# Attention's value product: values stationary in column groups, float32 probabilities moving

## The reference

```
def xattn(q, k, v, ...):            # q = layernorm(x), k = v = ctx; B=4, T=512
    q, k = rms_norm(q), rms_norm(k)
    # 16 query heads, 4 key/value heads (groups of 4 heads), head width 32; rotary embedding
    scores = einsum('bgnqd,bgkd->bgnqk', qg, k) / sqrt(32)
    scores = where(causal, scores, -1e30)
    attn = softmax(scores, axis=-1)
    out = einsum('bgnqk,bgkd->bgnqd', attn, v)
    return out @ w_out.T
x = x + xattn(layernorm(x), ctx)
x = x + ffn(layernorm(x))           # router, top 4 of 128 experts mixed from 8 bases, shared part
```

## Time and profile before

| | us |
|---|---|
| median of 3 runs (lowest, highest) | 987.56 (986.49, 988.49) |
| the profiled execution | 985.09 |
| its span in the trace | 983.3 |
| busy: PE, PEld | 863.3, 695.6 |
| busy: DVE, ACT, POOL | 566.4, 373.6, 355.8 |

### The profile page before, as it was taken

How to read it: one execution, slowest core, us unless ns; L and a number is a source line. 1 busy time by engine, 2 the same in 40 slices (tenths; PEclk the granted TensorE clock), 3 DMA queues, 4 the chain that set the end, 5 groups by cost and what they waited for, 6 DMA issues and landing times.

```text
span 983.3 us, 15430 instructions
## 1 busy us (share of the span) xinstructions
PE 863.3 (88%) x5008; PEld 695.6 (71%) x5008; DVE 566.4 (58%) x1406; ACT 373.6 (38%) x700; POOL 355.8 (36%) x384
## 2 busy tenths in 40 slices
PE   0488868986989986479999999999999999999998
PEld 0256656775777765368888888888888887888886
DVE  4487999899898876457644434343343434333332
ACT  1046867685687784155322212122121212111111
POOL 5746988778887334000012222222222220000000
PEclk9998988998997996879999999999999999999999
DMA  6311231231231200101011101010110100000000
GB/s 176 78 45 42 71 106 42 59 91 32 55 73 39 77 2 0 54 1 44 1 42 66 43 1 43 1 43 1 44 43 1 43 1 11 22 25 30 22 33 33
DMA packets 32814, 40.28 MB, mean 41 GB/s; under 512 B 6496, under 2 KB 19424, under 8 KB 32736
## 3 DMA queue, kind: packets, MB, share of 16 engines
q1 hardware_dynamic: 32736, 39.29, 13.9%
HBM read 19.08 MB, written 4.19 MB: 24 GB/s over the span
## 4 chain that ended last, share of the span: by engine, by line
PE 70%; DVE 14%; issue 7%; SPq 3%; ACT 2%; DMA 2%; POOL 1%; DVEq 0%; ACTq 0%; POOLq 0%
PE pair L1366 22%; PE bank L1366 22%; PE bank L1430 7%; PE bank L1308 5%; PE bank L1240 3%; DVE bank L940 3%; DVE p_l L959 3%; PE bank L1287 3%; SPq L378 2%; PE bank L1389 1%; SPq L365 1%; DVE mx L940 1%; PE pair L1255 1%; PE bank L1377 1%; PE bank L1444 1%
## 5 line engine op out<-in xcount | busy, mean ns | idle before, releaser
L645 POOL TENSOR_TENSOR macc<-macc,gb 128x256 f32<-128x256 f32 x112 | 85.8, 766 | 317.9 <-DVE gb L1160 317.9
L1240 PE MATMUL bank<-k_st,q_st 96*128 96x256 f32 (+2 forms) x256 | 98.2, 438 | 48.4 <-DVE mx L940 42.7
L940 DVE CUSTOM_DVE_ANT_0 bank<-bank,mask_qk 128x128 f32<-128x128 f32 (+3 forms) x256 | 121.1, 507 | 21.2 <-PE bank L1240 19.8
L1366 PE MATMUL pair<-w_h,t_h 128*128 128x512 f32 x320 | 126.7, 396 | 0.0
L1366 PE MATMUL bank<-w_h,t_h 128*128 128x512 f32 x320 | 126.6, 396 | 0.0
L1366 PE MATMUL pair<-w_l,t_h 128*128 128x512 f32 x320 | 125.7, 393 | 0.0
L1366 PE MATMUL bank<-w_l,t_h 128*128 128x512 f32 x320 | 125.6, 393 | 0.0
L1366 PE MATMUL pair<-w_h,t_l 128*128 128x512 f32 x320 | 125.6, 393 | 0.0
L1366 PE MATMUL bank<-w_h,t_l 128*128 128x512 f32 x320 | 125.6, 393 | 0.0
L959 DVE TENSOR_TENSOR p_l<-p,p_h 128x896 f16<-128x896 f32 x96 | 109.2, 1143 | 0.0
L1147 DVE SCALAR_TENSOR_TENSOR ga<-th,pair 128x256 f32<-128x256 f32 x80 | 33.6, 420 | 126.5 <-ACT th L800 126.5
(11 more groups left out here) (178 smaller groups left out, 1858.2 us busy)
## 6 DMA issues: line engine op xcount, KB each, us to landing
q_st<-turned_h SPq DMA_DIRECT2D x128, 64.0 KB, 2.0
q_st<-turned_l SPq DMA_DIRECT2D x64, 64.0 KB, 2.0
raw<-in_L_ffn_w_gate SPq DMA_DIRECT2D x16, 256.0 KB, 2.8
raw<-in_L_ffn_w_up SPq DMA_DIRECT2D x16, 256.0 KB, 3.6
out<-x SPq DMA_DIRECT2D x16, 256.0 KB, 2.0
x<-in_x SPq DMA_DIRECT2D x3, 1024.0 KB, 5.8
k_st<-turned_h SPq DMA_DIRECT2D x32, 64.0 KB, 2.0
ct<-in_ctx SPq DMA_DIRECT2D x4, 256.0 KB, 2.9
```

Of the source, the lines that this page charges most:

```text
L645: e.tensor_tensor(macc[:, g, :], macc[:, g, :], gb[:, i % 2, :], ALU.add).then_inc(s_acc, 1)
L940: e.tensor_tensor_reduce(s[:, 0:width], s[:, 0:width], mask_qk[:, T - width:T], 1.0, -3e38, ALU.add, ALU.max, mx[:, c % 2, t, j:j + 1]).th ...
L1240: e.matmul(a_bank[i % 2][:, 0:w], q_st[0:MAXROW, c % QR, j, t * P:(t + 1) * P], k_st[0:MAXROW, c % KR, 0:w], start=True, stop=True).then_i ...
L1366: last = e.matmul(g_bank[n % 4][:, 0:2 * I], t[:, k, cols], ww[:, k, :], start=(k == 0 and m == 0), stop=(k == KC - 1 and m == 2))
```

## The change

The probabilities are kept in float32 and not split. V, also float32 and straight from the loaded context, is the stationary operand, 128 keys x 32 columns, and the probabilities move, up to 512 columns at a time. The four heads of a group write four different quarters of the partitions of one bank, so the result comes out already turned; `combine` and `turn_out` are gone. The product is made once for a group of four heads, in one piece of 16 matmuls, at tick (c + 1) * G + 1. The row sums come from pass A: after the row minimum (scores now carry the sign and the scale, so minima stand for maxima) ScalarE takes the exponential of the score tile in its bank with an accumulator. The bank is free only then; there are three instead of two. The reciprocals are spread over 32 columns each by GpSimd, turned by TensorE, copied out by ScalarE, and multiplied on VectorE. Projections alternate between two banks and stand two to a tick. The context of all batches is loaded once, at the start, with x.

```diff
-LOW_BEHIND = 1
-PV_BEHIND = 2
+PV_TICK = 1
+    AR = 3
+    PW = G * (XW + YW + P)
+    def prob_at(k, j):
+        return (j * XW, j * XW + T, G * XW + j * YW, G * (XW + YW) + j * P)[k]
-        a_bank = bank[0:2]
-        b_bank = bank[2]
-        v_bank = bank[3]
+        a_bank = bank[0:3]
+        b_bank = bank[3]
+        o_bank = bank[5]
+            for b in range(2, B):
+                load_ctx(b)
+                load_x(b)
...
+            def out_low(c):       # GpSimd
+                e.tensor_tensor(o_l[:, kv, :], att[:], f32(o_h[:, kv, :]), ALU.subtract).then_inc(s_ol, 1)
+            def spread_inverse(c):
+                e.tensor_copy(heads(rrep[:]), rinv[:, c % 2].unsqueeze(3).broadcast_to([P, TT, G, D])
+                              ).then_inc(s_rrep, 1)
...
-            def exps(n, name):
+            def row_sum(n, t):    # ScalarE
+                s = a_bank[i % AR][:, 0:width]
+                e.wait_ge(s_max, i + 1)
+                e.activation(s, s, ACT.Exp, bias=mx[:, c % 2, t, j:j + 1], scale=-1.0,
+                             accum_out=sums[:, c % 2, t, j:j + 1]).then_inc(s_sum, 1)
+            def inverse_out(c):
+                e.activation(r_t[:, c % 2, :], m_bank[0][:], ACT.Copy).then_inc(s_rout, 1)
+            def exp_x(n):
+                e.activation(pr[:, c % 2, j * XW:(j + 1) * XW], pair[:, 0:XW], ACT.Exp, scale=-1.0
+                             ).then_inc(s_ex, 1)
+            def exp_y(c, y):
+                e.activation(pr[:, c % 2, at:at + T], b_bank[:], ACT.Exp, scale=-1.0).then_inc(s_ey, 1)
-            def value_rows(n):
+                if 0 <= n < NH:
+                    exp_x(n)
+                if 0 <= ahead < NH:
+                    row_sum(ahead, 0)
+                    row_sum(ahead, 1)
...                 # turned_high
+                if 0 <= n < NH and n % G < 3:
+                    exp_y(n // G, n % G)
+                if 0 <= ahead < NH:
+                    row_sum(ahead, 2)
+                    row_sum(ahead, 3)
+                for c in range(NC):
+                    if n == c * G + AT["maxima_turned"] + 1:
+                        inverse_out(c)
+                    if n == (c + 1) * G + PV_TICK:
+                        out_high(c)
...             # VectorE: maxima_split moves to the start of the next tick
+                e.wait_ge(s_sum, (c + 1) * G * TT)
+                e.reciprocal(rinv[:, r], sums[:, r]).then_inc(s_rinv, 1)
-            def low_rows(n, name):
+            def attended(c):
+                e.tensor_tensor(att[:], o_bank[:], r_t[:, c % 2, :], ALU.mult).then_inc(s_att, 1)
...             # TensorE
-                if i >= 2:
-                    e.wait_ge(s_max, i - 1)
+                if i >= AR:
+                    e.wait_ge(s_sum, i - AR + 1)
+            def pass_by(c, y):    # part y of two heads (y < 2) or four, 512 columns, and its mask
-            def value_product(n):
+            def value_product(c):
+                e.wait_ge(s_ex, c * G + G)
+                e.wait_ge(s_ey, c * 3 + 3)
+                for k in range(TT):
+                    for j in range(G):
+                        at = prob_at(k, j)
+                        last = e.matmul(o_bank[j * D:(j + 1) * D, k * P:T],
+                                        ct[:, b, k, kv * D:(kv + 1) * D], pr[:, r, at:at + T - k * P],
+                                        start=(k == 0), stop=(k == TT - 1))
-            def turn_out(c):
+                if 0 <= n < NH and n % G < 3:
+                    pass_by(n // G, n % G)
+                for c in range(NC):
+                    if n == (c + 1) * G + PV_TICK:
+                        value_product(c)
+                    if n == c * G + AT["maxima_turned"] + 1:
+                        inverse_turn(c)
+                ...             # pass_a(ahead, 2), pass_a(ahead, 3)
-                    if n == (g // TT + 1) * HB + AT["project"] + g % TT:
+                    if n == (g // TT + 1) * HB + AT["project"] + g % TT // 2:
                         project(g)
```

More of the change, by code:

```diff
@@ L54, in attention_and_mixture_kernel @@
     QR, KR = 3, 8
[L55 to L59, removed]
+    AR = 3
+    XW = T + T - P
+    YW = T - 2 * P
+    PW = G * (XW + YW + P)
     NB = KV + 1
@@ L95, in attention_and_mixture_kernel, with size_of, place @@
-        es = sb("es", [NE, 4])
-        cst = sb("cst", [P, 16])
+        def size_of(table):
+            bytes_of = {F32: 4, F32R: 4, BF16: 2}
+            return sum(-(-bytes_of[dt] * math.prod(shape[1:]) // 32) * 32 for _, shape, dt in table)
+        def place(stack, table, size=None):
+            got = [stack.enter_context(nc.sbuf_tensor(name, shape, dt)) for name, shape, dt in table]
+            gap = 0 if size is None else size - size_of(table)
+            if gap:
+                stack.enter_context(nc.sbuf_tensor(table[0][0] + "_pad", [P, gap // 4], F32))
+            return got
@@ L130, in attention_and_mixture_kernel @@
[L130 to L142, removed]
@@ L170, in attention_and_mixture_kernel @@
[L170 to L181, removed]
@@ new lines, in attention_and_mixture_kernel @@
+        early = max(size_of(att_early), size_of(ffn_early) + shared)
+        middle = max(size_of(att_middle), size_of(ffn_middle))
+        late = max(size_of(att_late), size_of(ffn_late))
+        att_mem = ExitStack()
+        (cos_t, sin_t, junk, wq_b, wk_b, xc, ct, stats, mv, ssk, sc, csq, rw_b, r1_b, r2_b, turned_h,
+         turned_l) = place(att_mem, att_early, early)
+        (ident16, mask_kq, mask_qk, q_st, k_st, mx, sums, rinv, mhl, m_t, pr) = place(
+            att_mem, att_middle, middle)
@@ L621, in pool_engine @@
                         rope(b, 0)
-                    if n == b * HB + AT["values"]:
-                        values(b)
                 for c in range(NC):
+                    if n == c * G + AT["maxima_split"] + 1:
+                        spread_inverse(c)
                     if n == c * G + AT["rope_queries"]:
                         rope(c // KV, c % KV + 1)
-                if 0 <= low < NH and low % G < 2:
-                    low_rows(low)
-                for c in range(NC - 1):
-                    if n == c * G + AT["combine"]:
-                        combine(c)
+                    if n == (c + 1) * G + PV_TICK:
+                        out_low(c)
                 if n == AT["router_weights"]:
@@ L1292, in turn_out @@
-            def turn_out(c):
-                e.wait_ge(*normed(c))
-                e.wait_ge(*m_free[1])
-                for t in range(TT):
-                    last = e.transpose(m_bank[1][:, t * P:(t + 1) * P], att[:, t, :], ident[:])
-                last.then_inc(s_ot, 1)
-                m_free[1] = (s_ol, c + 1)
+                    e.wait_ge(s_ex, n)
+                for k in range(2):
+                    dst = pair[:, k * T:k * T + T - k * P]
+                    e.matmul(dst, k_st[:, c % KR, k * P:(k + 1) * P], q_st[:, c % QR, j, k * P:T],
+                             start=True, stop=True)
+                    last = e.matmul(dst[:, 0:P], ident16[:], mask_kq[:], start=False, stop=True,
+                                    skip_group_check=True)
@@ L1307, in project @@
                     for m, (o, w) in enumerate(((o_h, wo_h), (o_h, wo_l), (o_l, wo_h))):
-                        last = e.matmul(m_bank[1][:], o[:, k, rows], w[:, k, :], start=(k == 0 and m == 0),
+                        last = e.matmul(m_bank[g % 2][:], o[:, k, rows], w[:, k, :], start=(k == 0 and m == 0),
                                         stop=(k == KC - 1 and m == 2))
                 last.then_inc(s_proj, 1)
-                m_free[1] = (s_x1, g + 1)
+                m_free[g % 2] = (s_x1, g + 1)
             for n in ticks:
-                ahead, product = n + LEAD, n - PV_BEHIND
+                ahead = n + LEAD
                 for c in range(NC):
```

444 lines of the change are left out of this document (147 added, 297 removed).

## The result

The changed kernel takes 1020.9 us, median of 4 runs (1019.5 to 1023.0), against 987.0 us before (985.0 to 988.5): ratio 1.035, 95% interval 1.032 to 1.037. Forecast was 993 us. So the sign was right and the size was not: +34 us where I had +5. By the prediction's own chances (slower 0.52, faster 0.42) the sign was little more than a toss. The profiled execution took 1023.0 us with a span of 1021.2.

What follows compares the result with a forecast made beforehand. VectorE was taken to bound attention before the change, ScalarE after it. Body +18.5, tail -12, last projections -3.4 and start +2 gave +5: 990 us profiled, 993 us as median; range 952 to 1045 us.

Steps and rivals of the forecast that it cites:

- the clock term: At each of three batch boundaries in attention, the lower clock after the stalls was to add 1.2 us.
- V: Length of a group's value product on TensorE, taken as 2.3 us.
- V - 1.0: In each group, ScalarE's stall behind the value product: its length less 1.0 us, near 1.3 us.
- dear rate: TensorE price taken from the slowest twelve projection matmuls: 5.16 us, 0.43 us each.
- Case A: Whole kernel slightly slower, with a value product near 2.3 us: 993 us, chance 0.40.
- the price of V: Each us of value product length costs the kernel 16 us (15 groups and the last product).
- ScalarE's floor: ScalarE's work in an undisturbed attention group, which becomes its bound: 15.5 us.
- the boundaries: Three batch boundaries in attention add 15.3 us each, 46 in all, for statistics, projections, waits and clock.
- The tail: Last m_t to the first projection of the last batch: 22.6 us against 34.5, so -12.
- E: Ring or clock worse (1 us more stall a head, lower clock held): +25 us on any case, chance 0.06.
- B: Value product overlaps only in part, or not at all at the cheap rate: 4.6 us, kernel 1030 us, chance 0.16.
- D: Value product below 2.0 us, short enough to hide behind the exponentials: kernel 974 or 966 us, chance 0.32.

Runs made afterwards that it cites:

- filler run: Changed kernel plus sixteen unused bf16 matmuls before the third scores of a head, in three ticks of four: 1005.8 us, 1.019 of before.
- head by head order: Changed kernel with the sixteen matmuls of each value product ordered by head instead of by key block: 1097.2 us (one run).
- the pieces: Changed kernel with the value product in four pieces by key block, spread over two ticks: 985.5 us, 0.9996 of before.

## Why the forecast was right in sign and wrong in size

**What failed: the clock term.** I had "the lower clock after the stalls 1.2" once per batch boundary, and V at one value everywhere. By the timeline the body from first to last m_t took 408.59 - 53.91 = 354.7 us against 320. Undisturbed groups take 20.43 to 20.47 instead of 18.2: 15 x 2.27 = 34 us, all of the body's miss. Of the 2.27, the wait behind the product has 2.0 (3.30 against V - 1.0 = 1.3): 1.3 because the product is longer, 0.7 because less of it is hidden than the 1.0 of the rule. Rows 1 held the hint: the stretch with the granted clock of 0.80 was the one in which TensorE was busy 17.4 of 25 us, the one with 1.00 had 20.4. The change takes TensorE's bf16 products between all scores away and leaves it waiting in each group, which is the 0.80 case made regular, and I priced it as an accident of boundaries. (Busy shares can't be compared across clock levels: a projection matmul is recorded with 0.63 us at half clock and 0.39 at full, so the 19.15 of 25 us at 0.68 can't be set against 17.4 at 0.80.) The second hint was in the earlier trace rows. The twelve matmuls of 5.16 us, which I took for a "dear rate", stand behind a wait of 1.50 us, and the granted clock of before says what they are:

```profile
389.00:393.00 4.00, 4.00 (x10) 3.13 (x11) 0.00 (x0) 1.19 (x3) 0.00 (x0) 0.50 0.00 0
```

Case A with this term right would have been 993 + 34 = 1027; of the 6 us that this is too high, about 5 are that the median here lies 2.1 us below the profiled execution, where I had put it 2.5 above.

**Right in number, by luck in its working: V at full clock.** I had 2.3 us, "the dear rate, four abreast", and at full clock it is 2.29. But that rate was one of half clock, where a product takes 4.43 us (filler run, from 247.04 us). What one matmul of this kind takes alone at full clock no run shows: with the four of a head behind one another the product comes to 6.87 us, not to the 8.6 of the dear rate. So the number came right from a row that does not bear on it. The Trainium skill, "TensorE: Matmul & The Clock Gate", Part 3, has matmuls start and end strictly in program order; read for pairs in one column group that gave 4.3 us, and the trace of after disagrees. The head by head order, three times slower, fits a strict order without proving it.

**Right within 0.7 us: the price of V.** The stall rule V - 1.0 gives 1.3, 2.6 and 6.8 for the measured 1.51, 3.30 and 7.09. What is hidden is 0.78 us where the product has full clock (2.29 and 1.51, 6.87 and 6.09) and 0.3 to 0.7 where it begins at half clock (3.62 and 3.30, 4.43 and 4.07, 7.76 and 7.09); why it is less there is open. Head by head the mean group grew by 27.69 - 23.65 = 4.0 us, 61 of the 76 us; most of the rest is in the tail's two products.

**Right: ScalarE's floor.** 15.4 us of work in a group against 15.5. A row sum of 512 columns is 0.66 + 0.19 recorded and 0.68 from start to start, of 128 columns 0.35: about 0.86 ns a column and 0.24 us, where I had 0.87 and 0.28. turned_low's wait is 0.81 against 0.9. Heads without exp_y and the split together 0.96 against 0.5. With the clock held all through (filler) the whole group is 18.12 against 18.2.

**Right only in sum: the boundaries.** Over 20.47 each, the boundary groups add 0.9 + 16.2, 0.9 + 16.2 and 11.8 = 46 us, the forecast's 46. Its parts were not right. The statistics' group adds 0.9 us where I had 3.6 + 1.0: ScalarE waits 1.63 us for them, as squares and moments now take 3.5 us instead of 5.7 (the squares 287 ns each on the mean, where the earlier trace rows had 1.37 us for the first), and its wait behind the product is 0.8 shorter (2.46), that product having more of the full clock. The projections cost 11 us a batch, not 8. Two causes are read from the trace and not tested apart: half clock (a first projection of 5.25 us), and the wait for m_bank[0] (2.33 us), which I missed because I followed the queue of TensorE and not who frees the bank.

**The tail and the FFN.** Last m_t to the first projection of the last batch: 427.37 - 408.59 = 18.8 us against 22.6 forecast and 34.5 before. From that projection to the end of the span it is 593.8 us against 594.3; up to the FFN's first turn 4.1 us came, by the alternating banks (3.4 forecast), and the FFN, which I took as it is, gave 3.6 back. Start: first m_t at 53.9 against 53.0.

**Rivals.** E named the lower clock held and gave it +25: on A that is 1018, 3 us from the result and the nearest of all, with the least chance (0.06, as C) and without a working. B's sign "above 23 us of mean spacing" is what came (23.65), and its time of 1030 was the next, but its mechanism, no overlap at the cheap rate, is not what happened. D's view, that the product must be short enough to hide, is right for the pieces: 17.3 us a group at best and 985 us with two small edits.

## What to carry to other kernels

When a change takes steady small work from TensorE and gives it back in one block, price the block at half clock unless the engine is kept busy before it; look at the granted clock of the stretch that is as idle as the new one will be, and of every row whose time you take as a price. In a ring of banks a block costs its length less a small cover (0.3 to 0.8 us here), so cut it into pieces between single tiles before asking for a shorter one. A bank shared by several users needs its own list of who frees it last.

## What the runs showed of the hardware

- Sixteen float32 matmuls in four column groups (5120 columns) take 2.29 us at full clock when neighbours are of different groups (4.43 with the granted clock at 0.50), and 6.87 at full clock when the four of a group follow each other. The Trainium skill, "FP8 and Floating Point Precision", TensorE Precision Notes, has float32 at four passes; 5120 x 4 / 2.4 GHz = 8.5 us serial would be an estimate by it, above the 6.87 measured at full clock, so no run here shows it.
- The granted clock fell from 1.00 to 0.50 behind waits of TensorE of 1.4, 1.6 and 0.7 us with work between them; with filler in such waits it stayed at 1.00 in the same group. Useless matmuls can pay: filler of about 0.85 us a tick at full clock took 15 us off the changed kernel.
- Float32r matmuls of the FFN in steady state came 431 or 432 between 650 and 750 us in the nine kernels of the changed layout and 436 before, at full granted clock in all and with the same FFN code. With a shift by 32 bytes it is 430. The cause is open.
